# Two transformer layers on one core: the causal mask of the second attention goes from a TensorE matmul to the VectorE instruction that finds the row maximum

## The reference

```python
scores = jnp.einsum('bhqd,bhkd->bhqk', q, k) / math.sqrt(HD)
scores = scores * scale          # 0.5 for keys 0..34, 1.5 for 35..106, rows >= 107 only
causal = jnp.where(qpos[:, None] >= kpos[None, :], 0.0, jnp.finfo(jnp.float32).min)
probs = jax.nn.softmax(scores + causal, axis=-1)
attn = jnp.einsum('bhqk,bhkd->bhqd', probs, v)
```

## Time and profile before

| what | us |
|---|---|
| median of 3 runs | 1886.32 |
| lowest and highest | 1885.12, 1891.42 |
| span of the profiled execution | 1888.9 |

### The profile page before, as it was taken

The page is one execution under the profiler, slowest core; times in us unless marked ns, Lnnn a source line. Parts: engine busy times, 40 slices in busy tenths (PEclk is TensorE's granted clock), DMA queues, the critical chain, the costliest instruction groups (busy, mean ns, idle before and its releaser), DMA issues. The chain is left out here.

```text
span 1888.9 us, 34715 instructions
## 1 busy us (share of the span) xinstructions
PE 1762.9 (93%) x11225; PEld 1302.0 (69%) x11225; DVE 1209.3 (64%) x2244; ACT 720.0 (38%) x1534; POOL 715.2 (38%) x837
## 2 busy tenths in 40 slices
PE   4988999999978999999999999999999999899998
PEld 3643343333856887887878878878878878777776
DVE  7778888744476676676676676676576676533434
ACT  4424555567014514515515415425325325311111
POOL 3002422115055355354254265255364362323432
PEclk9988999999989999999999999999999999999999
DMA  5000000000020000001001001001001010011101
GB/s 135 1 1 2 2 1 2 2 2 12 1 71 23 18 18 24 18 17 29 12 17 35 7 17 35 6 18 40 1 19 39 12 36 19 15 50 33 39 24 45
DMA packets 30600, 42.39 MB, mean 22 GB/s; under 512 B 11397, under 2 KB 12549, under 8 KB 30453
## 3 DMA queue, kind: packets, MB, share of 16 engines
q1 hardware_dynamic: 30474, 40.55, 7.8%
HBM read 38.25 MB, written 2.10 MB: 21 GB/s over the span
## 5 line engine op out<-in xcount | busy, mean ns | idle before, releaser
L1454 DVE TENSOR_TENSOR ptnl<-ps,ptnh 128x512 fp32r<-128x512 f32 (+1 forms) x320 | 204.0, 638 | 135.3 <-ACT ptnh L1372 129.8
L1372 ACT ACTIVATE ptnh<-ps 128x512 fp32r<-128x512 f32 (+1 forms) x320 | 177.6, 555 | 268.3 <-PE ps L1298 265.3
L68 PE MATMUL ps<-xth,wh 128*128 128x512 f32 (+1 forms) x560 | 223.6, 399 | 1.6 <-DVE xtl L148 1.6
L668 ACT ACTIVATE pt<-ps 128x512 f32<-128x512 f32 x288 | 171.8, 597 | 137.8 <-PE ps L483 86.3
L70 PE MATMUL ps<-xth,wl 128*128 128x512 f32 (+1 forms) x560 | 221.3, 395 | 0.0
L69 PE MATMUL ps<-xtl,wh 128*128 128x512 f32 (+1 forms) x560 | 221.3, 395 | 0.0
L976 POOL TENSOR_TENSOR wl<-wl,onehot 128x256 f32 (+1 forms) x128 | 93.9, 734 | 327.8 <-DVE onehot L800 318.1
L816 DVE TENSOR_REDUCE negm<-ps 128x128 f32 (+14 forms) x256 | 184.5, 754 | 45.0 <-PE ps L461 40.7
L1442 DVE TENSOR_REDUCE negm<-ps 128x1 f32<-128x768 f32 (+3 forms) x224 | 183.6, 820 | 36.5 <-PE ps L1276 33.8
L68 PE MATMUL ps<-ptnh,vh 128*128 128x256 f32 x576 | 183.7, 319 | 10.2 <-DVE ptnl L1454 9.7
L70 PE MATMUL ps<-ptnh,vl 128*128 128x256 f32 x576 | 161.3, 280 | 0.0
(11 more groups left out here) (221 smaller groups left out, 3982.2 us busy)
## 6 DMA issues: line engine op xcount, KB each, us to landing
raw<-in_w SPq DMA_DIRECT2D x48, 256.0 KB, 2.6
raw<-in_wo SPq DMA_DIRECT2D x32, 256.0 KB, 2.6
raw<-in_gate_main SPq DMA_DIRECT2D x10, 256.0 KB, 2.8
raw<-in_up_main SPq DMA_DIRECT2D x10, 256.0 KB, 2.7
raw<-in_down_main SPq DMA_DIRECT2D x10, 256.0 KB, 2.8
resid<-in_x SPq DMA_DIRECT2D x4, 512.0 KB, 5.2
out<-resid SPq DMA_DIRECT2D x8, 256.0 KB, 2.0
wl<-in_wq SPq DMA_DIRECT2D x1, 1024.0 KB, 8.1
```

The source lines that it names most:

```text
L68: pe.matmul(out, lh, rh, start=first, stop=False)
L668: nc.scalar.activation(pt[:, at, :], ps[:, TB[at], :], ACT.Exp).then_inc(exp_done, 1)
L1372: nc.scalar.activation(ptnh[:, i % PT_RING, 0:w], ps[:, b, 0:w], ACT.Copy).then_inc(high_ready, 1)
L1454: nc.vector.tensor_tensor(ptnl[:, i % PT_RING, 0:w], ps[:, b, 0:w], ptnh[:, i % PT_RING, 0:w].bitcast(F32), ALU.subtract).then_inc(low_rea ...
```

## The change

The mask matmul goes; the last product of `qk` raises `qk_filled`. A buffer `ramp`, 1024 columns in chunks 4 and 5 of `keep["raw"]`, holds zeros and in its last 128 columns the mask. VectorE's `tensor_reduce` becomes `tensor_tensor_reduce`: it adds the last `(t + 1) * 128` columns of `ramp` to the scores, multiplies by -1, writes the result back where the scores lay (PSUM, or `pbuf` for t = 0), and takes the row minimum into `negm`. It follows a semaphore increment of its own queue, which takes over the wait. The exponential reads the negated scores with `scale=-1.0`. Two instructions ahead of the normalisation fill `ramp`. SP loads chunks 4 and 5, and what is queued behind them, only after the last row maximum.

```diff
+        ramp = keep["raw"][:, 4:6, :].rearrange("p b c -> p (b c)")
...
             for j in range(2):
                 for which in range(3):
+                    if 3 * j + which == 4:
+                        sp.wait_ge(max_ready, KV1 * NHEADS)
                     load_chunk(sp, a, keep["raw"], j, j, which, P, next_in[j])
...
-                    products(pe, out[:, c0:c0 + w], q, k, True, c0 + BLK < width)
-                pe.matmul(out[:, t * P:(t + 1) * P], identb[:], masku[:], start=False, stop=True).then_inc(qk_filled, 1)
+                    last = products(pe, out[:, c0:c0 + w], q, k, True, True)
+                last.then_inc(qk_filled, 1)
...
-                    nc.scalar.activation(pbuf(n), src, ACT.Exp, bias=negm[:, n:n + 1], accum_out=rowsum[:, n:n + 1]).then_inc(exp_ready, 1)
+                    nc.scalar.activation(pbuf(n), src, ACT.Exp, bias=negm[:, n:n + 1], scale=-1.0, accum_out=rowsum[:, n:n + 1]).then_inc(exp_ready, 1)
...
+            nc.vector.memset(ramp[:, 0:S - P], 0.0).then_inc(ramp_ready, 1)
+            nc.vector.tensor_copy(ramp[:, S - P:S], masku[:]).then_inc(ramp_ready, 1)
             norm.vector(nc, dve, None)
...
+            dve.wait_ge(ramp_ready, 2)
...
                     if t:
-                        nc.vector.tensor_reduce(negm[:, i:i + 1], qk_banks(i)[:, 0:(t + 1) * P], AX.X, ALU.max, negate=True).then_inc(max_ready, 1)
+                        scores = qk_banks(i)[:, 0:(t + 1) * P]
                     else:
                         free_probabilities(dve, i, gg)
-                        nc.vector.tensor_tensor(pbuf(i), qk_banks(i)[:, 0:P], tscale[:], ALU.mult).then_inc(max_step, 1)
+                        scores = pbuf(i)
+                        nc.vector.tensor_tensor(scores, qk_banks(i)[:, 0:P], tscale[:], ALU.mult).then_inc(max_step, 1)
                         dve.wait_ge(max_step, gg * 4 + FIRST_TILE.index(i) + 1)
-                        nc.vector.tensor_reduce(negm[:, i:i + 1], pbuf(i), AX.X, ALU.max, negate=True).then_inc(max_ready, 1)
+                    dve.sem_inc(dve_waited, 1)
+                    nc.vector.tensor_tensor_reduce(out=scores, in0=scores, in1=ramp[:, S - (t + 1) * P:S], scale=-1.0, scalar=3e38,
+                                                   op0=ALU.add, op1=ALU.min, accum_out=negm[:, i:i + 1]).then_inc(max_ready, 1)
```

More of the change, by code:

```diff
@@ L1119, in layer1 @@
         next_in = [sem(f"next_in{i}") for i in range(3)]
-        k0_init, waited = sem("k0_init"), sem("waited")
+        k0_init, waited, dve_waited, ramp_ready = sem("k0_init"), sem("waited"), sem("dve_waited"), sem("ramp_ready")
         block = ctx.enter_context(nc.Block())
```

## The result

The changed kernel takes 1909.65 us (median of 4 runs, 1908.07 to 1910.68) beside 1888.86 for the kernel before in the same series: ratio 1.0114, 95% interval 1.0094 to 1.0133. It is slower by 1.1%; the forecast was 1873, and 1909.65 lies above the range too.

What follows compares the result with a forecast made beforehand. TensorE's own sequence was taken to bound the attention loop. -25.6 for the masks, +1.0 and +4.6 lost to waits, +3.1 latency, +2.2 queue, +1.1 filling gave -13.6: 1873 us, own range 1862 to 1881, full range 1861 to 1900.

Steps and rivals of the forecast that it cites:

- The clock: TensorE's lower clock behind the eight group ends: 1.5 us per stretch, up to 12 us either way, sign left open.
- more waits than 39 us: Sign of a wrong forecast: TensorE's weight loads wait longer in all for the exponential or the subtraction than 39 us.
- What the removal is worth: Mask matmuls leaving TensorE's sequence in the attention loop: 25.6 us, less 1.0 and 4.6 lost to waits, leaving 20.0.
- one mask inside each of the 38 waits: Where `av` waits for its subtraction, removal only lengthens the wait: 38 x 0.12 = 4.6 us of the gain lost.
- half rate: Rival: VectorE needs two passes a column with two f32 sources and accumulation; +21 us, 1907 us; chance 0.14.
- Reading the accumulator: VectorE, after each maximum: 0.16 us for fetching the second result, bounds 0 and 0.20.
- The increment: VectorE's semaphore increment carrying the wait ahead of each maximum: taken as 0, range 0 to 0.20 us.
- The filling of `ramp`: VectorE's memset and copy ahead of the normalisation, delaying everything behind: 1.1 us, bounds 0.5 and 1.4.
- SP's wait: Chunk loads held until the last maximum land by 1635.1, hidden behind output projection ending at 1640.0; costs nothing.
- the latency: Scores to exponential 0.10 us longer at 31 TensorE waits: 3.1 us, bounds -2.2 and 10.5.
- the queue: Subtractions queued behind longer maxima on VectorE: 13 x 0.17 = 2.2 us, bounds 0 and 15.6.
- the latency eats it: Rival: each maximum 0.34 us longer, TensorE's slack spent; -3.1, 1883 us. No change 0.18; slower, some 1895, 0.08.

## Why the prediction was wrong

The four runs with both loops written out split the change without a stop for code at a turn. Each step is a difference of two medians, good to some 3 us. In us: taking the matmuls away, 1887.14 to 1875.29, -11.8; VectorE's part, to 1890.96, +15.7; the fetches at the turns, to the changed kernel's 1909.65, +18.7. The sum is +22.5; the prediction's was -13.6.

**No term for the code of VectorE's loop.** This is the step that failed most, with 18.7 us where the sum has nothing: the change was costed by durations and queues, and the 64 instructions that it adds to each turn (32 increments, 32 readings of the accumulator) only by their time. Their room turned the sign. The Trainium skill has the rule, in "Runtime: NRT & Kernel Launch", section "Instruction fetch mechanics": an engine other than TensorE holds 32 KiB of code, 512 instructions, and a taken branch to code that is no longer held stops the engine until it has been fetched. The traces agree with the stop, 2.2 to 2.4 us each, and the positions fit the sum: three blocks of 128 for the loop and one fetched ahead stay, four and one don't. They show packets of 8 KB where the page has blocks of 16.

**The clock.** "Up to 12 us either way, in practice a third of that" was too small. By the measure above the changed kernel loses 61.6 us and the same kernel with both loops written out 47.5, so up to 14 of the 18.7 are clock: in the windows shown a gap of TensorE at the turn is followed by a stretch at 0.50. The rest would be the gaps themselves, not measured apart. Two of the signs named for a wrong forecast came: more waits than 39 us, and more time at half clock. The group's period, which was to fall by 1.5 to 2 us, rose: between 136.0 and 137.5 us before, between 139.4 and 140.5 after.

**What the removal is worth.** The 25.6 us of places on TensorE were read nearly rightly: over all 145 places ahead of an `av` the mask's mean is 0.10 us (0.408 to 0.305 from the last product to the second matmul behind it) for the 0.12 of the one place read, which makes some 23 in all. But 5.6 were to be lost to waits and 13.8 were (25.6 - 11.8), or some 11 of the 23. The step "one mask inside each of the 38 waits" charged only the waits that stood there; others had slack of under a mask, which the run without masks shows as 54.

**What the instruction costs.** The durations were right, and half rate is refuted at 1232 ns, and for the first tiles, with both sources in SBUF, by the 0.29 us of 20 of them. The prediction's 798 ns for two sources in SBUF was a mean of 0.69 us alone and up to 1.76 beside GpSimd, so the second source costs next to nothing by itself. Reading the accumulator takes 133 ns but begins 0.08 us before the instruction's end, and the exponential starts 0.10 after that end, so 0.16 was too much. The increment, put at 0 "as VectorE mostly has something queued", costs 0.16 us at each start where VectorE waits for the scores; 0.20 was kept for the range and was the truer end. The first tiles, where scaling is followed by a second pass that waits for the first and can fall beside GpSimd, had no term. Leaving the increment and the first tiles out takes 8.6 us off (1890.96 to 1882.37), although 32 mask matmuls come back with it. By their share of the 11.8 (28 of 32 tiles, 10.3) VectorE's part is then some 5.5 us, an estimate. That this is near the forecast's 6.4 is luck, since the filling below is a larger part of it than was forecast.

**The filling of `ramp`.** Its two rows take 0.97 us, and the square root behind them waits 1.40 for 0.37, 1.03 more, as forecast. But the sign that the prediction named, the first transpose of `layer1` 1.1 us later, didn't come: it starts 3.56 us behind the block's first memset in the kernel before and 6.76 in the changed one, 3.2 later, and 5.77 to 6.92 in all runs that fill `ramp`. The later start puts the normalisation's small operations beside GpSimd's two-source operation, and there one of 0.17 us takes 1.12. The term was mis-sized by some 2 us. First the changed kernel, then the kernel before:

```profile
521.00 0.81 DVE L1414 MEMSET raw<- 128x896 f32 x1
521.72 0.16 DVE L1415 CAST raw<-masku 128x128 f32<-128x128 bf16 x1
...
522.67 0.21 ACT L168 ACTIVATE l_sd<-l_veps 128x8 f32<-128x8 f32 x1 [1.40 <-DVE l_veps L130]
...
523.52 1.26 POOL L1501 TENSOR_TENSOR wl<-raw,wh 128x512 fp32r<-128x512 f32 x1
523.69 1.12 DVE L140 TENSOR_SCALAR l_t<-l_t 128x8 f32<-128x8 f32 x1
...
527.06 1.75 PE L163 MATMUL ps<-identf,xn 128*128 128x128 f32 x7 [12.75 <-DVE xn L152]
```

```profile
527.27 0.17 DVE L140 TENSOR_SCALAR l_t<-l_t 128x8 f32<-128x8 f32 x1
...
528.60 1.12 PE L163 MATMUL ps<-identf,xn 128*128 128x128 f32 x4 [9.55 <-DVE xn L152]
```

**SP's wait** stays hidden, as forecast: its last issue ends at 1648.26, the last transfers land some 2.7 us after their issue, and the last sum of the residual ends at 1658.70.

```profile
1647.43 0.83 SPq L1227 DMA_DIRECT2D araw<-in_down_a  x1
...
1658.01 0.69 DVE L1481 TENSOR_TENSOR resid<-ps,resid 128x512 f32<-128x512 f32 x1 [2.11 <-PE ps L70]
```

The narrow range of 1862 to 1881 doesn't follow from the bounds beside it either: with -2.2 to 10.5 for the latency and 0 to 15.6 for the queue they give 1865 to 1894, and 1909.65 lies above that too.

Of the rivals, "the latency eats it" named the size of what is left when the fetches are gone (+3.8 without them); none had the fetches. Open stay: why VectorE's mask in the 12 middle tiles alone costs more than in 28, and what decides whether TensorE's loop is fetched again.

## What to carry to other kernels

Before adding instructions to an engine's loop, count what one turn executes, register operations included, and see from the instruction queue's packets whether the loop still stays in place; if not, write the loop out for that engine or move it. A removed instruction of the bound engine is worth its slot only where nobody else is nearly late, and leaving it out of the kernel for one run prices that directly. An idle stretch that the profile puts down to an engine that had long finished is worth a look at the code fetches. A mean over a group of instructions can hide two kinds; what runs beside the slow ones tells them apart.

## What was not expected of the hardware

A packet of VectorE's code is 8 KB, some 128 instructions, and a miss at a branch cost 2.2 to 2.4 us. One-time filler moved the time by 25 us (58 increments, kernel before) and by -14 (78, changed kernel, against its own 1909.65). TensorE's loop is fetched again as well, 9 packets of 16 KB a group in the kernel before, with its first transposes never idle there; without the mask matmuls there were 2 packets from 700 to 1560 us, for the kernel before's 56. A VectorE instruction that reads two sources in SBUF took up to 1.32 us for 0.29 while GpSimd ran a two-source operation, and one that reads PSUM took no longer.
